# Two spectra that share a table are added on GpSimd, and TensorE multiplies the two sums in place of the four spectra

## The reference, cut to what matters

```
x = x + attention(layernorm(x), context)            # 2048 context rows per sequence
u = layernorm(x)
k_f = rfft(k, n); u_f = rfft(u, n, axis=1)
x = x + irfft(k_f * u_f, n)[:, :128] + u * D        # a long convolution along the tokens
x = x + experts(layernorm(x))                       # one of 8 experts per token, 512 -> 2048 -> 512
```

## Time and profile before

| what | value |
|---|---|
| median of three runs | 335.52 us (333.64 to 336.96) |
| profiled execution | 335.69 us, its span 333.9 us |
| PE, DVE, ACT, POOL busy | 296.2, 216.6, 157.9, 44.7 us |
| mean granted clock of TensorE | 0.963 of full speed |
| last matmul before to_time (TensorE) | until 131.6 us |
| spectra, to_time, gate logits | 130.7 to 157.6 us |
| routing, sorting | 157.6 to 172.6 us |
| experts' loop | 172.6 to 333 us |

### The profile page before, as it was taken

The page is one execution under the profiler, slowest core; times in us unless marked ns, Lnnn a source line. Parts: engine busy times, 40 slices in busy tenths (PEclk is TensorE's granted clock), DMA queues, the critical chain, the costliest instruction groups (busy, mean ns, idle before and its releaser), DMA issues.

```text
span 333.9 us, 7456 instructions
## 1 busy us (share of the span) xinstructions
PE 296.2 (89%) x2542; PEld 167.3 (50%) x2542; DVE 216.6 (65%) x505; ACT 157.9 (47%) x300; POOL 44.7 (13%) x64
## 2 busy tenths in 40 slices
PE   0999999999999997998979999899999999679530
PEld 0864657585879863456654444444444444215100
DVE  0896895788994755786877665566665666505510
ACT  3987998896841220022026453455444554404320
POOL 1270000000000000010000112121112211111203
PEclk9989999999999999999999999999999999969965
DMA  8999968509975059900009956999946999999910
GB/s 183 374 404 322 391 267 283 222 16 375 355 259 223 32 186 427 399 4 9 0 32 384 422 188 215 416 420 417 414 181 247 414 422 412 414 417 429 409 44 2
DMA packets 18888, 92.08 MB, mean 276 GB/s; under 512 B 3601, under 2 KB 6289, under 8 KB 9138
## 3 DMA queue, kind: packets, MB, share of 16 engines
q1 hardware_dynamic: 15570, 89.59, 67.0%
q0 software_dynamic: 1664, 2.10, 3.9%
q10 hardware_dynamic: 1632, 0.11, 0.4%
HBM read 89.69 MB, written 2.36 MB: 276 GB/s over the span
## 4 chain that ended last, share of the span: by engine, by line
PE 70%; DMA 16%; ACT 5%; DVE 4%; issue 2%; POOL 1%; ACTq 1%; SPq 0%; DVEq 0%; POOLq 0%
PE bank L1522 15%; DMA ring<-in_w 14%; PE bank L1535 13%; PE bank L1330 8%; PE bank L1311 8%; PE bank L1340 4%; ACT ring L514 3%; PE bank L1291 3%; PE bank L1376 2%; PE bank L1319 2%; PE bank L1383 2%; DMA cols<-in_times 2%; PE bank L1490 1%; PE bank L1354 1%; PE bank L1491 1%
## 5 line engine op out<-in xcount | busy, mean ns | idle before, releaser
L1522 PE MATMUL bank<-ring,small 128*32 128x256 f32 x1200 | 68.6, 380 | 1.8 <-ACT small L721 1.1
L1535 PE MATMUL bank<-ring,hbuf 128*32 128x512 f32 x424 | 53.8, 628 | 9.6 <-DMA ring<-in_w 9.5
L1522 PEld LDWEIGHTS bank<-ring,small 128*32 128x32 f32 x1200 | 39.0, 110 | 35.9 <-issue 7.0
L1179 DVE SCALAR_TENSOR_TENSOR tab<-bank,cols,tab 32x512 f32<-32x512 f32 x20 | 14.8, 739 | 48.3 <-ACT tab L699 48.3
L707 ACT ACTIVATE hbuf<-hbuf 128x128 f32<-128x128 f32 x76 | 23.5, 309 | 30.6 <-DVE hbuf L1162 30.6
L1535 PEld LDWEIGHTS bank<-ring,hbuf 128*32 128x32 f32 x424 | 13.6, 112 | 41.3 <-issue 30.9
L699 ACT ACTIVATE tab<-bank,cols 32x512 f32<-32x512 f32 x20 | 13.6, 679 | 39.5 <-PE bank L1535 37.9
L1311 PE MATMUL bank<-ring 128*128 128x512 f32 x64 | 29.7, 594 | 0.0
L1330 PE MATMUL bank<-ring 128*128 128x256 f32 x128 | 28.4, 379 | 0.0
L1240 POOL DMA_INDIRECT out<-y_pair,cols x20 | 26.7, 1333 | 10.4 <-issue 10.4
L1330 PEld LDWEIGHTS bank<-ring 128*128 128x128 f32 x128 | 24.3, 190 | 4.9 <-issue 1.9
(11 more groups left out here) (203 smaller groups left out, 434.4 us busy)
## 6 DMA issues: line engine op xcount, KB each, us to landing
ring<-in_w SPq DMA_DIRECT2D x58, 1024.0 KB, 14.7
ring<-in_ctx_turned SPq DMA_DIRECT2D x4, 2048.0 KB, 11.1
ring<-in_ctx SPq DMA_DIRECT2D x4, 2048.0 KB, 12.4
work<-in_w SPq DMA_DIRECT2D x4, 1024.0 KB, 14.6
x_ext<-in_w SPq DMA_DIRECT2D x2, 1024.0 KB, 17.4
ring<-in_wq_t SPq DMA_DIRECT2D x4, 256.0 KB, 7.1
x_ext<-in_x SPq DMA_DIRECT2D x4, 256.0 KB, 7.3
x_ext<-in_bv POOLq DMA_DIRECT2D x4, 256.0 KB, 11.9
```

Source lines behind the costliest of these rows:

```text
L1179: ins = dve.scalar_tensor_tensor(out=y_sum, in0=bank[0:TW, Y_BANK, :], scalar=prob_now[0:TW], in1=y_sum, op0=ALU.mult, op1=ALU.add)
L1522: ins = pe.matmul(bank[j * TW:(j + 1) * TW, H_BANK[s], 0:HN], xw[:, d, :], first_layer(e, s, k)[:, d % 2, j * HN:(j + 1) * HN], start=d == ...
L1535: ins = pe.matmul(bank[j * TW:(j + 1) * TW, Y_BANK, :], h_t[s][:, (CT * c + j) * TW:(CT * c + j + 1) * TW], second_layer(e, s, c)[:, j, :] ...
```

## The change

After the DVE reads of a sequence, POOL adds cos2 to cos1 and sin2 to sin1, in place, one 128x512 add each, and signs each off on a new semaphore, spectra_ready. to_time waits for the first sum, multiplies it by cos_t, waits for the second and multiplies it by sin_t: two matmuls in place of four. The reads by DVE, PE's order and all other engines stay. In POOL's list the adds of sequences 0 and 1 come behind root 5 and ahead of root 6, those of 2 behind root 6, those of 3 behind root 7.

```diff
+            def spectra_added(b):
+                after_read(pool, ("uc", b))
+                after_read(pool, ("us", b))
+                cos1, cos2, sin1, sin2 = spectra[b % 2]
+                pool.tensor_tensor(cos1, cos1, cos2, ALU.add).then_inc(spectra_ready, 1)
+                pool.tensor_tensor(sin1, sin1, sin2, ALU.add).then_inc(spectra_ready, 1)
-            for k in range(1, 2 * NB + 1):
-                inverse_root(k + 1)
+            inverse_root(2)
...
+            inverse_root(5)
+            spectra_added(0)
+            spectra_added(1)
+            inverse_root(6)
+            spectra_added(2)
+            inverse_root(7)
+            spectra_added(3)
+            inverse_root(8)
+            inverse_root(9)
...
             def to_time(b):
-                after_read(pe, ("uc", b))
-                after_read(pe, ("us", b))
                 dst = may_fill(pe, ("y", b))
-                cos1, cos2, sin1, sin2 = spectra[b % 2]
-                pe.matmul(dst, table("cos_t"), cos1, start=True, stop=False)
-                pe.matmul(dst, table("cos_t"), cos2, start=False, stop=False)
-                pe.matmul(dst, table("sin_t"), sin1, start=False, stop=False)
-                did_fill(pe.matmul(dst, table("sin_t"), sin2, start=False, stop=True), ("y", b))
+                pe.wait_ge(spectra_ready, 2 * b + 1)
+                pe.matmul(dst, table("cos_t"), spectra[b % 2][0], start=True, stop=False)
+                pe.wait_ge(spectra_ready, 2 * b + 2)
+                did_fill(pe.matmul(dst, table("sin_t"), spectra[b % 2][2], start=False, stop=True), ("y", b))
```

More of the change, by code:

```diff
@@ L333, in perceiver_layer @@
         xn2_hi_ready, xn2_lo_ready = sem("xn2_hi_ready"), sem("xn2_lo_ready")
+        spectra_ready = sem("spectra_ready")
         hot_ready, lsub_ready, lexp_ready = sem("hot_ready"), sem("lsub_ready"), sem("lexp_ready")
@@ L1226, in _ @@
                 pool.dma_start(x_sb[:, b, :], bv.partition_broadcast(P), accum_op=ALU.add).then_inc(bias_added_to[b], 16)
-            for k in range(1, 2 * NB + 1):
-                inverse_root(k + 1)
+            def spectra_added(b):
[5 more added lines that the diff above has]
+            inverse_root(2)
+            inverse_root(3)
+            inverse_root(4)
+            inverse_root(5)
[7 more added lines that the diff above has]
+            inverse_root(9)
             pool.wait_ge(rows_written, 16 * NB)
```

## The result

The kernel after took 340.81 us in the median (338.49 to 344.39, four runs), the kernel before beside it 334.76: a ratio of 1.0152 [1.0097, 1.0208]. The forecast was 334.9, and the range ended at 337.6. The profiled execution took 339.25 us, with a span of 337.2 against 333.9. Executions of every kernel here, the one before too, spread over 6 us and more with TensorE's clock, and the ratios compare the least disturbed ones.

The account below looks back on a forecast made before the run. In the stretch PE was taken as nearly full, with DVE one or two microseconds behind. Walk -1.5 plus clock fall +0.9 gave -0.6: 335.69 to 335.1, less 0.17 for the median, 334.9 us; range 333.0 to 337.6.

Parts of the forecast that it names:

- What comes after moves with this stretch: Everything behind the routing start, up to the kernel's end, was to shift by the stretch's gain, counted at full size.
- the last burst of transfers: Last weight transfers, ending the kernel: they wait for places PE frees; forecast wrong if the burst starts as it did.
- The stretch: First spectrum read to first routing instruction, 130.67 to 157.55 us, PE and DVE both nearly full; forecast change -0.6 us.
- the walk: Step-by-step timing of the stretch's reads, adds, matmuls and DVE work with 1.05 us an add: ends 1.5 us earlier.
- 0.4 per tenth: Sensitivity of the walk's end: each tenth of a microsecond in an add's length is worth about 0.4 us.
- fall once, for 0.9: PE idles 2.74 us around the first to_time; its clock halves for one matmul, costing 0.9 us.
- time in hand: A later clock fall would mostly meet the microsecond that y1 and y2 have spare; none counted in the forecast.
- PE's 6.9 us: Eight removed to_time matmuls at 0.86 us each; only 1.5 us come through because DVE's work is untouched.
- Rival 2: POOL paces the stretch: adds of 1.46 us, walk +0.1, clock falls 0.9 and about 0.6; 335.6 to 337.1 us, chance 0.24.
- Rival 1: In the stretch the clock does not fall and adds are cheap: walk -1.5 to -3.0, 332.5 to 334.0 us, chance 0.20.
- Rival 3: In the stretch an add takes 2.1 us or more, delaying the tail: 339 to 340 us, chance 0.08.
- Rival 4: PE is the bound of the stretch after all and all 6.9 us come back: 328.6 us, chance 0.03.

Follow-up runs that it names:

- e2: Changed kernel with eight two-column matmuls ahead of the first to_time, so TensorE's code is as long as before; ratio 1.0032 to the kernel before, no pause.
- e8: Changed kernel with eight two-column matmuls at the very end of TensorE's program, behind the experts' loop; ratio 1.0135 to the kernel before, pause of 1.59 us.
- e10: Kernel before without eight of its nine keep_warm matmuls, nothing of the change, loop eight matmuls earlier; ratio 1.0189 to the kernel before, with the pause.
- e11: Changed kernel with four two-column matmuls ahead of the first to_time, loop four matmuls earlier than in the kernel before; ratio 1.0029 to it, no pause.
- e4: Changed kernel with eight unread 256-column matmuls spread over three TensorE waits, code as long as before; ratio 0.9997 to the kernel before, clock 1.00.
- e9: Kernel before with its four matmuls; GpSimd makes the eight adds into an unread place and TensorE doesn't wait; ratio 1.0012 to the kernel before.
- e6: Half the change: GpSimd adds only the cosine pair while TensorE multiplies both sine spectra, three matmuls; ratio 0.9980 to the kernel before.
- one-sum version: GpSimd adds only the cosine pair, three matmuls instead of the kernel before's four; five runs, some with filler matmuls, ratios 0.9966 to 1.0041 to it.
- e1: The changed kernel run again unaltered as control; ratio 1.0083 to the kernel before, with the pause.
- e13: e6 repeated word for word; ratio 1.0041 to the kernel before, no pause.

## Why the prediction was wrong, point by point

**The step that failed** is in its second paragraph: "What comes after moves with this stretch ... I count a gain here at its full size". What comes after did not move with it. The experts' loop lost 2.6 us of its own, because removing instructions moved its code. The prediction named one way in which the end might not move (the last burst of transfers) and did not look at the instruction queue, though it stands in the page's list of queues. e2, e8, e10 and e11 show it from four sides: the pause goes when the loop's place in the code is given back, in whole or by half, stays when the padding comes behind the loop, and appears in a kernel without the change. That the late packet is what PE waits for is inferred from the four pauses, which all end 2.2 to 2.4 us after its start; no run delayed the packet alone. The Trainium skill (Runtime: NRT & Kernel Launch, section "Instruction fetch mechanics") says that the sequencer fetches its code in blocks of 16 KiB through a queue of its own, mostly hidden, and that a taken branch to a page that isn't there stalls. The size agrees (twelve packets, 0.20 MB). In the loop up to 262 us, "mostly hidden" holds for the packet behind the late one, at 219.66 us, beside which PE has no wait; the stall itself came 28 matmul records into a round of the loop.

**The stretch: -0.6 forecast, +0.81 measured.** Its two terms were right in kind, and the first was 1.1 us too kind.
- The walk said -1.5 with adds of 1.05 us; they took 1.26. By the prediction's own 0.4 per tenth that makes -0.7. Measured without a fall (e4): -0.43. Against the walk, e4 has its first L929 0.45 us later after the first read (6.33 and 5.88), which is the two longer adds, and 0.65 more from the third to the fourth (4.49 and 3.84): there the first add takes 1.44, L1039 1.14 for 0.69, and root 8, which the walk let end 0.54 us behind the adds, takes 0.99. The other estimate that it gave, 1.12 from the Trainium skill (GPSIMD Engine Reference, section 3.1), was nearer and still short.
- The clock was to fall once, for 0.9. It fell twice, to 0.50 each time: after PE had waited 3.09 us, and again between 144 and 148, after waits of 1.35 and 0.56. The first cost 1.3 us at L929 (e4 against after), both together 1.24 at the routing, since the second met time in hand, as was said. -0.43 and +1.24 are the +0.81. In e2 and e11 it fell once and 1 us later after the first read, and the stretch is 0.89 and 0.90 us longer than in e4: there the forecast's 0.9 was met.

**Right:** PE's 6.9 us are not the gain, because DVE stands behind; L929 of sequences 1 to 3 start without a wait, the first two at the intervals of the walk (4.60 and 4.66 us against 4.61; the last 4.43 against 3.84); the reads of the spectra are not held up; adds beside DVE cost little (e9: 0.04 us). Rival 2 came nearest in number: the change without the pause (e2 and e11) has ratios of 1.0032 and 1.0029, which on the 335.52 us of before are 336.6 and 336.5, inside its 335.6 to 337.1. Of its terms the falls came (two in after, one each in e2 and e11), but not the adds that use up the walk's gain. The forecast's own range holds these times too, so the pause is what took the time out of it; a small gain was not there even so. Rivals 1, 3 and 4 are out: an add is 1.26 us, not 0.63 or 2.1, and PE waits.

**The sum as it should read:** -0.6, and 1.07 for the walk and 0.34 for the clock, is the +0.81 of the stretch; 2.57 for the pause and 0.27 at the last weights, less the 0.36 by which the stretch began earlier, make +3.3, which is what the spans of the profiled executions differ by.

## What to carry to other kernels

Taking instructions out of an engine moves all its code behind them, and a loop far away may then wait for a piece of its own code: after a change in the number of instructions, look for "issue" in the chain and for the instruction queue in the DMA view, and test with the same number of trivial instructions put back, ahead of the loop and behind it, before the change itself is judged. Where a second engine stands close behind the one that is relieved, price the wait for the relieving engine and not its work (e9 against after), and give the relieved engine other work while the sum is made (e6, whose stretch was shorter, though its time is not shown to be). When work is taken from TensorE, read its granted clock again: in after its falls took more than the stretch gained (1.24 us against 0.43), in four of five traces of the one-sum version most of it.

## What the runs showed of the hardware that was not expected

- TensorE stops for 1.6 to 2.2 us beside a late 16 KB instruction packet, while weights stream at 384 to 402 GB/s, and goes on 2.2 to 2.4 us after the packet's start (after, e1, e8, e10). With the loop four matmuls earlier (e6, e11, e13) or in its old place there is no such stop.
- A 128x512 float32 add on GpSimd takes 1.26 us. Beside it DVE's L1039, with both inputs in SBUF, takes 1.06 to 1.15 us in place of 0.69; its reads of PSUM keep their 0.68.
- The clock fell after PE had waited 3.09 us, 2.22 (e11), or 1.33 behind matmuls of two columns (e2), and not in e4, where it waited 1.27 behind matmuls of 256 columns. Between 150 and 160 us it falls in one execution of a kernel and not in another (e13 and e6), though the wait ahead of it is the same, 0.78 us.
